# Sparse cross-attention: the list count and the negated maximum computed by VectorE, and a constant scale in the first Relu

## The reference, cut to what matters

```python
def _L3_xattn_ref(x, knowledge_embeddings, Wq, bq, Wk, bk, Wv, bv, Wo, bo):
    ...
    Q = _split_heads(x @ Wq.T + bq, N_HEADS)                      # 16 heads of 8
    K = _split_heads(knowledge_embeddings @ Wk.T + bk, N_HEADS)
    V = _split_heads(knowledge_embeddings @ Wv.T + bv, N_HEADS)
    scores = jnp.einsum('bhsd,bhnd->bhsn', Q, K) / SCALE
    topk_scores, topk_indices = jax.lax.top_k(scores, 32)
    sparse_weights = jax.nn.softmax(topk_scores, axis=-1)
    sel_V = jnp.take_along_axis(V[:, :, None, :, :], topk_indices[..., None], axis=3)
    context = jnp.einsum('bhsk,bhskd->bhsd', sparse_weights, sel_V)
    ...
    return context @ Wo.T + bo
```

## Time and profile before

| | us |
|---|---|
| median of three runs | 4340.24 |
| lowest, highest | 4337.01, 4341.01 |
| the profiled execution | 4350.81 |
| its span | 4349.1 |

### The profile page before, as it was taken

One profiled execution on the slowest core, in us unless ns is written; L12 is line 12 of the kernel. 1 busy time (PEld: TensorE's weight loads), 2 busy tenths in 40 slices (PEclk: granted clock), 3 DMA queues, 4 the chain that ended last, 5 costly groups with the idle time before them and its releaser, 6 DMA issues. The chain is left out here.

```text
span 4349.1 us, 71120 instructions
## 1 busy us (share of the span) xinstructions
PE 3502.9 (81%) x25855; PEld 2825.6 (65%) x25855; DVE 3269.0 (75%) x5198; ACT 2819.1 (65%) x4654; POOL 1440.0 (33%) x1185
## 2 busy tenths in 40 slices
PE   6445749999999788999999985777777777777787
PEld 3334337999999566899999852555555555555676
DVE  4675877777777633877787656999999999899644
ACT  3112616666666434666666543999999999999832
POOL 0000503111210201121111012677777777767510
PEclk9555859999999888999999987999999999999988
DMA  8743011111110121111111001000000000000000
GB/s 276 107 60 108 4 41 41 37 31 39 39 31 16 24 64 36 31 39 31 31 39 31 9 20 41 16 16 16 16 31 16 16 16 31 16 16 8 1 23 18
DMA packets 186344, 161.32 MB, mean 37 GB/s; under 512 B 7996, under 2 KB 174092, under 8 KB 185996
## 3 DMA queue, kind: packets, MB, share of 16 engines
q1 hardware_dynamic: 182604, 142.83, 12.5%
q10 hardware_dynamic: 3392, 13.93, 0.9%
HBM read 127.36 MB, written 20.20 MB: 34 GB/s over the span
## 5 line engine op out<-in xcount | busy, mean ns | idle before, releaser
L559 PEld LDWEIGHTS psU<-ctxN,ST 128*128 128x128 f32 x6656 | 852.5, 191 | 98.4 <-issue 39.7
L559 PE MATMUL psU<-ctxN,ST 128*128 128x129 f32 x6656 | 866.8, 275 | 20.7 <-issue 20.7
L645 ACT ACTIVATE ST<-ST 128x512 f32<-128x512 f32 (+1 forms) x832 | 513.2, 625 | 165.5 <-DVE ST L747 161.2
L947 PE MATMUL psU<-ctxN,PT 128*128 128x129 f32 (+1 forms) x3328 | 430.3, 280 | 206.3 <-ACT PT L1061 206.3
L1196 DVE MAX8 top<-pairs 128x8 f32<-128x1602 f32 (+1 forms) x384 | 588.0, 1535 | 0.1
L1151 POOL TENSOR_TENSOR P<-P,EX 128x1601 f32<-128x1601 f32 x128 | 460.0, 3594 | 381.9 <-ACT P L1053 381.9
L747 DVE TENSOR_TENSOR ST<-ST,psB 128x512 f32<-128x512 f32 (+1 forms) x832 | 556.3, 677 | 2.7 <-PE psB L578 2.7
L733 DVE TENSOR_TENSOR psA<-psA,ST 128x512 f32<-128x512 f32 x640 | 446.6, 698 | 137.6 <-ACT ST L637 69.7
L947 PEld LDWEIGHTS psU<-ctxN,PT 128*128 128x128 f32 (+1 forms) x3328 | 393.2, 192 | 230.6 <-ACT PT L1061 230.6
L547 PE MATMUL psS<-statL,ctxH 128*128 128x512 f32 x832 | 393.0, 472 | 6.2 <-ACT ST L637 2.9
L925 PE MATMUL psS<-KT,stat 128*128 128x512 f32 (+1 forms) x1024 | 381.9, 515 | 16.7 <-DVE maxes L1174 15.9
(11 more groups left out here) (509 smaller groups left out, 6755.1 us busy)
## 6 DMA issues: line engine op xcount, KB each, us to landing
ctxN<-in_ctx SPq DMA_DIRECT2D x48, 768.0 KB
ahead_ctxT<-ctxT_scratch SPq DMA_DIRECT2D x32, 800.5 KB, 4.4
ctxT_scratch<-trn ACTq DMA_DIRECT2D x16, 800.5 KB
ctxT<-ctxT_scratch SPq DMA_DIRECT2D x16, 800.5 KB, 6.2
nat<-in_ctx SPq DMA_DIRECT2D x16, 768.0 KB
dist_scratch<-dd SPq DMA_DIRECT2D x8, 800.5 KB
skewed<-in_ctx SPq DMA_DIRECT2D x8, 768.0 KB
ctx_late<-in_ctx SPq DMA_DIRECT2D x8, 768.0 KB
```

The lines of the kernel that those rows point to most:

```text
L559: last = pe.matmul(psU[:, q, 0:D + 1], ST[0:n, i % SLOTS, q * 128:q * 128 + 128], ctxN[0:n, j, k, 0:D + 1], start=(k == 0 and q % 2 == 0), ...
L645: act.activation(ST[0:n, i % SLOTS, :], ST[0:n, i % SLOTS, :], ACT.Exp).then_inc(exp_done, 1)
L947: last = pe.matmul(psU[:, 0:D + 1], PT[0:w, t % 2, k, :], ctxN[0:w, t // TB % 2, k, 0:D + 1], start=(k == 0), stop=(k == NC - 1))
```

## The change

The negation of the maximum and the count over the 32 listed values go from ScalarE to VectorE, as `tensor_scalar` instructions on one column and on 32 columns. The negation stands in VectorE's step s behind find(s-1, 2) and ahead of drop(s, 0). The count now sums "greater than the edge" (a positive number, where the sum of signs was its negative), stands at the end of VectorE's step, behind the fold, and belongs to tile s-1. GpSimd's formulas change sign accordingly. The first Relu of `mark` is scaled by the constant 1601 in place of `span`; at the edge `sides` is 0, so the scale matters on the two other sides alone, where both values end as `span` and 0.

```diff
--- before.py
+++ after.py
@@ -819,7 +819,7 @@
         above = c.sb(st, "above", [128, 2])
         below = c.sb(st, "below", [128, 2])
         sides = c.sb(st, "sides", [128, K])
-        listed_sides = c.sb(st, "listed_sides", [128, TOPK])
+        listed_above = c.sb(st, "listed_above", [128, TOPK])
         span = c.sb(st, "span", [128, 2])
         rest = c.sb(st, "rest", [128, 2])
         li = c.sb(st, "li", [128, 2])
@@ -1011,13 +1011,6 @@
                         act.wait_ge(exp_done, t - 2 + ONE)
                     act.activation(SS[:, t % 3, 0:K], psS[:, 0:K], ACT.Copy).then_inc(copied, 1)
 
-                def negate(t):
-                    act.wait_ge(listed_early, EARLY * t + 1 + ONE)
-                    if t >= 2:
-                        act.wait_ge(exp_done, t - 1 + ONE)
-                    act.activation(mneg[:, t % 2:t % 2 + 1], top[:, t % 3, 0:1], ACT.Copy, scale=-1.0
-                                   ).then_inc(max_ready, 1)
-
                 def exps(t):
                     act.wait_ge(max_ready, t + 1 + ONE)
                     if t >= 2:
@@ -1036,10 +1029,6 @@
                         act.wait_ge(rest_ready, t - 1 + ONE)
                     act.activation(sides[:], SS[:, t % 3, 0:K], ACT.Sign, scale=-1.0, bias=edge,
                                    accum_out=below[:, j:j + 1]).then_inc(sided, 1)
-                    if t:
-                        act.wait_ge(counted, t + ONE)
-                    act.activation(listed_sides[:], top[:, t % 3, :], ACT.Sign, scale=-1.0, bias=edge,
-                                   accum_out=above[:, j:j + 1]).then_inc(counted, 1)
 
                 def mark(t):
                     j = t % 2
@@ -1047,7 +1036,7 @@
                     act.wait_ge(sided, t + 1 + ONE)
                     if t >= 2:
                         act.wait_ge(turned, 4 * (t - 1) + ONE)
-                    act.activation(P[:, j, :], sides[:], ACT.Relu, scale=span[:, j:j + 1], bias=rest[:, j:j + 1]
+                    act.activation(P[:, j, :], sides[:], ACT.Relu, scale=float(K), bias=rest[:, j:j + 1]
                                    ).then_inc(graded, 1)
                     act.wait_ge(graded, t + 1 + ONE)
                     act.activation(P[:, j, :], P[:, j, :], ACT.Relu, scale=-1.0, bias=span[:, j:j + 1]).then_inc(marked, 1)
@@ -1098,7 +1087,6 @@
                         copy_weights(s - 3, 2)
                         copy_weights(s - 3, 3)
                     if 0 <= s - 1 < T:
-                        negate(s - 1)
                         exps(s - 1)
                     if s >= 4:
                         copy_ut(s - 4)
@@ -1135,14 +1123,14 @@
                     pool.wait_ge(sided, t + 1 + ONE)
                     if t >= 2:
                         pool.wait_ge(marked, t - 1 + ONE)
-                    pool.tensor_scalar(span[:, j:j + 1], above[:, j:j + 1], 2.0, below[:, j:j + 1], ALU.mult, ALU.subtract
+                    pool.tensor_scalar(span[:, j:j + 1], above[:, j:j + 1], -2.0, below[:, j:j + 1], ALU.mult, ALU.subtract
                                        ).then_inc(spanned, 1)
                     pool.wait_ge(spanned, 2 * t + 1 + ONE)
                     pool.tensor_scalar(span[:, j:j + 1], span[:, j:j + 1], float(K), None, ALU.add
                                        ).then_inc(spanned, 1)
                     pool.wait_ge(spanned, 2 * t + 2 + ONE)
                     pool.tensor_scalar(rest[:, j:j + 1], span[:, j:j + 1], -float(TOPK), above[:, j:j + 1],
-                                       ALU.add, ALU.subtract).then_inc(rest_ready, 1)
+                                       ALU.add, ALU.add).then_inc(rest_ready, 1)
 
                 def weigh(t):
                     j = t % 2
@@ -1205,6 +1193,24 @@
                     dve.match_replace(left, top_t[:, 8 * n:8 * n + 8], maxes[:, t % 2, :] if n == 0 else left, LOW
                                       ).then_inc(listed_early if n < 2 else listed_late, 1)
 
+                def negate(t):
+                    dve.wait_ge(listed_early, EARLY * t + 1 + ONE)
+                    if t >= 2:
+                        dve.wait_ge(exp_done, t - 1 + ONE)
+                    dve.tensor_scalar(mneg[:, t % 2:t % 2 + 1], top[:, t % 3, 0:1], -1.0, None, ALU.mult
+                                      ).then_inc(max_ready, 1)
+
+                def count_above(t):
+                    j = t % 2
+                    dve.wait_ge(listed_early, EARLY * (t + 1) + ONE)
+                    dve.wait_ge(listed_late, LATE * (t + 1) + ONE)
+                    if t:
+                        dve.wait_ge(counted, t + ONE)
+                    if t >= 2:
+                        dve.wait_ge(rest_ready, t - 1 + ONE)
+                    dve.tensor_scalar(listed_above[:], top[:, t % 3, :], top[:, t % 3, TOPK - 1:TOPK], None, ALU.is_gt, ALU.add,
+                                      accum_out=above[:, j:j + 1]).then_inc(counted, 1)
+
                 def inverse(t):
                     dve.wait_ge(u_ready, t + 1 + ONE)
                     if t >= 2:
@@ -1226,6 +1232,7 @@
                     if late:
                         find(s - 1, 2)
                     if early:
+                        negate(s)
                         drop(s, 0)
                     if late:
                         drop(s - 1, 2)
@@ -1241,6 +1248,8 @@
                         add(*summed[s - 3])
                     if s + 1 < T:
                         fold(s + 1)
+                    if late:
+                        count_above(s - 1)
                 inverse(T - 1)
                 for g in range(PARTS):
                     add(NT - 1, g)
```

## The result

The changed kernel takes 4361.69 us in the median (4357.85 to 4366.92, 4 runs), the kernel before 4338.62 on the same chip: +23.1 us, ratio 1.0054, 95% interval [1.0037, 1.0072]. It is slower by more than the 0.2% that counts as a difference, and 4361.69 lies above the range of 4329 to 4358.

What follows compares the result with a forecast made beforehand. TensorE's path was taken to hold the score copy, ScalarE alone to decide behind it. Plain steps -7.0, additions +8.8, start +0.9 and end +0.5 gave +3.2 us: 4343.4 us, range 4329 to 4358.

Steps and rivals of the forecast that it cites:

- What bounds the kernel: Up to the score copy, TensorE's and ScalarE's paths run side by side, ScalarE's 0.23 us shorter; afterwards ScalarE alone decides.
- Removed from ScalarE: Negation and count, 0.63 us ahead of the score copy, gain nothing under TensorE's path; uncovered, 76 us over 121 steps.
- Constant scale: First Relu, behind norm: a constant scale makes it 0.098 us shorter in every step.
- The wait moves to the negation and VectorE slides: VectorE waits at the negation for the exponential, sliding about 3 us; step 10.66 us, 0.058 less, -7.0 over 121 steps.
- Count: List count on VectorE behind the fold: costs 0.15 us (0 to 0.23), off the path.
- The additions of y: VectorE's late addition delays TensorE's turn_u and values; 20 counted steps lose 0.44 us each, +8.8 us.
- Ends of the stage: First four steps at VectorE's pace, +0.9 us; last negation step +1.0 and the two behind it -0.5, together +0.5.
- (b): Rival: VectorE's path from negation to norm decides every step, the negation costing 0.17 us; +15.6, 4356 us, chance 0.16.
- (a): Rival: VectorE's slide is free, negation and hand-overs fit ahead of norm, turn_u has room; -10.5, 4330 us, chance 0.14.
- (c): Rival: VectorE's negation waits for GpSimd's weighing multiply at the port; some +180, 4520 us, chance 0.06.
- (d): Rival: ScalarE alone is the bound, so 0.63+0.098 us per step are gained; -88, 4252 us, chance 0.03.
- (e): Rival: the constant scale does not shorten the first Relu; +12 on the sum, 4355 us, chance 0.03.

Runs made afterwards that it cites:

- Experiment 7: Kernel before with TensorE's next scores issued between the second and third block of values: 4309.31 us against 4345.96.
- experiment 4: Kernel before with only the list count moved to VectorE behind the fold, with GpSimd's changed signs: 4340.43 us against 4340.56.
- experiment 2: Kernel before with only the constant scale in the first Relu: 4330.83 us against 4340.56.
- experiment 3: Kernel before with only the negation moved to VectorE, two columns: 4373.65 us against 4340.56.
- experiment 5: Whole change with VectorE's addition of y put right behind the reciprocal: 4345.25 us against 4345.96 for the kernel before.
- experiment 6: Whole change plus 16 unread TensorE transposes ahead of its wait in addition steps: 4342.10 us against 4345.96 for the kernel before.
- experiment 1: Whole change with a third column for the negated maxima: 4327.69 us against 4340.56 for the kernel before.

## Why the prediction was wrong

By its steps:

- **What bounds the kernel: right.** Experiment 7 shows the two paths side by side. Their distance was 0.33 us and not 0.23.
- **Removed from ScalarE, hidden: right.** ScalarE waits 0.77 us ahead of the score copy (0.86 foretold), and experiment 4 measures the count at -0.1 us. The worth that I gave it without the cover, 76 us, was about double: 121 x 0.35 = 42.
- **Constant scale: right.** 0.095 measured, 0.098 taken; alone it brings 9.7 us. The Trainium skill (ScalarE: Activation LUTs, What ACT_TABLE_LOAD costs) puts an operand that is one value per partition at about 93 ns; the trace agrees, with 95.
- **The wait moves to the negation and VectorE slides: right**, in place and size, and the chain negation, load, reciprocal, norm was the right one. It came out at A+6.27 instead of A+6.24. The negation's price was 0.07, under the 0.09 taken; the hand-over from the exponential was 0.11 (3412.98 to 3413.09), where I had taken the 0.04 of another pair. A plain step so came to 10.70 instead of 10.66, and the term of -7.0 was -0.7. Experiments 2 and 3 show both halves: -0.10 a step from the scale, +0.08 from the negation.
- **Count: right** that it is off the path; its price was not. Its main instruction lasts 0.24 us, where 0.15 at most was taken, but it starts in time that was free: the next maximum starts 1.06 us behind the fold's start, 1.03 before, so the count costs VectorE 0.03 us and not 0.15.
- **The additions of y: here it failed.** The lateness was right: turn_u foretold at A+9.17, measured at 2965.32, which is A+9.24 with norm at 2962.35; 20 steps that count, and just these 20 measured, the 9 cheap ones at 0.29 for my 0.44. But the step went on with "sixteen loads take 1.86", a row read while TensorE had hardly waited. It did not ask what 2.6 us of idle time do to the engine that waits. In 11 of the steps the clock fell and the price was 1.6 to 1.9 us. The term was +8.8 and measures 22.5, less 2.2 in the steps behind: +20.3. Another +0.3 is the one long step without an addition, which the sum had not; the same step takes 11.04 us in experiments 5 and 6 too, but not in 1 and 3, and its cause stays open. Experiments 5 and 6 take it away in two ways.
- **Ends of the stage:** foretold +0.9 and +0.5, measured +0.2 and +0.6. The last steps went as said (10.70 us where 9.62 was the earlier trace rows).

Sum by the same steps: -0.7 + 20.3 + 0.3 + 0.2 + 0.6 = +20.7 where I had +3.2. Of the rivals, (b) named a slower kernel, but by VectorE's path in every step, at 4356; that mechanism did not decide. None of the rivals had the clock in it. That the clock can fall in this stage, and what a fall costs, could have been read in the trace of before. One of its two steps of 13.45 us, timeline and then busy time of two stretches (the granted clock is the number before the last two):

```profile
2804.19 1.38 PE L947 MATMUL psU<-ctxN,PT 128*128 128x129 f32 x10 [1.72 <-ACT PT L1061]
...
2805.41 4.61 PE L925 MATMUL psS<-KT,stat 128*128 128x512 f32 x8
...
2810.05 1.50 ACT L1012 ACTIVATE SS<-psS 128x1601 f32<-128x1601 f32 x1 [1.92 <-PE psS L925]
```

```profile
2796.60:2800.60 4.00, 2.78 (x17) 1.77 (x17) 3.40 (x6) 3.74 (x6) 3.82 (x6) 1.00 1.05 346
...
2804.60:2808.60 4.00, 4.00 (x14) 2.04 (x13) 3.79 (x6) 3.53 (x6) 4.00 (x2) 0.63 0.00 0
```

Here TensorE had stood still for 1.72 us, the clock came to 0.63 in the stretch behind, the scores took 4.61 us instead of 2.91, and the score copy waited 1.92 us instead of 0.23. I had read one plain stretch, with a clock of 1.00, and no step that stood out. But these rows would not have told in which steps it falls: a plain step has a wait of 1.63 us at the same place and keeps its clock.
Rivals (a), (c), (d) and (e) are excluded: the slide was not free, no negation is released by GpSimd, ScalarE's 0.63 us brought nothing, the Relu got shorter.

The Trainium skill (TensorE: Matmul & The Clock Gate, What's actually happening) says that TensorE's clock has a full and a half rate and goes by how busy the engine has lately been. The trace agrees, with a granted clock of 1.00 behind the cheap wait and 0.50 in the slow part behind the costly one; I should have weighed it in the step that makes TensorE wait, where it spoke against the change.

## What to carry to other kernels

When a change makes one engine late, follow the lateness to each engine that waits, and price the wait there with what it does to that engine's speed: behind the wait TensorE can lose more than in it. Steps of before that are longer than their like show what such a fall costs, though not where it will come. Before moving an operation that recycles a small buffer, look at where its reader stands in the other queue; one more column, or a place a few instructions further down, made the same edit 11 to 13 us faster than before instead of 23 slower. And work taken off an engine brings nothing while another path ends at the same place: here the order of TensorE's queue was the lock, and worth more than all of the change.

## What was not expected of the hardware

- Waits of the same length do not cost the same. Of the 27 stalls of TensorE, those with 2.4 to 2.7 us of idle time were followed by 26 loads in 2.98 us in some steps and in 3.83 to 4.62 us in others. What of the engine's activity decided between them was not tried.
- An idle time in a row understates what goes with it: 0.23 us of wait was worth 0.33 a step.
- The step from an exponential's end on ScalarE to a waiting VectorE instruction took 0.11 us, from a reciprocal on VectorE to a waiting copy on ScalarE 0.03 (3416.97 to 3417.00).
- The counting instruction of VectorE lasts 238 ns and its accumulator read 84 ns, yet both together push the next maximum back by 0.04 us only: it starts 1.07 us behind the fold's start in experiment 4, and 1.03 in the kernel before.
- A lower clock does not always cost. Over the whole execution it is 0.903 in experiment 7 and 0.921 in most runs of the kernel before, and the kernel is 36.7 us faster all the same.
